# An attention kernel with sparse experts: visits of four value tiles beside six ring banks, the expert table shared with GpSimd, and expert down products one slot later

## The reference

```python
Q, K, V = heads(layernorm(x) @ W_Q), heads(ctx @ W_K), heads(ctx @ W_V)
attn = softmax(where(mask == 0, -1e9, Q @ K.T / sqrt(d)))
x = x + tanh(g0) * (merge(attn @ V) @ W_T)
h = layernorm(x)
w, sel = top_k(softmax(h @ router_w.T), 2)
y = sum over the two chosen experts e of w_e * ((silu(h @ gate_e) * (h @ up_e)) @ down_e)
x = x + tanh(g1) * y
```

## Time and profile before

| | us |
|---|---|
| median of 3 runs | 448.39 |
| lowest and highest run | 444.69, 450.77 |
| profiled execution | 447.15 |
| span of its trace, first to last instruction | 445.0 |

### The profile page before, as it was taken

How to read it: one execution, slowest core, us unless ns; L and a number is a source line. 1 busy time by engine, 2 the same in 40 slices (tenths; PEclk the granted TensorE clock), 3 DMA queues, 4 the chain that set the end, 5 groups by cost and what they waited for, 6 DMA issues and landing times. The chain is left out here.

```text
span 445.0 us, 10141 instructions
## 1 busy us (share of the span) xinstructions
PE 409.3 (92%) x3747; PEld 237.4 (53%) x3747; DVE 323.0 (73%) x698; ACT 273.3 (61%) x576; POOL 118.7 (27%) x260
## 2 busy tenths in 40 slices
PE   7887999999999999999999999999984877989996
PEld 3436455555564555555555555545532556666785
DVE  3980778677777899888889988888991662432786
ACT  3302656676776777777777777777761557645433
POOL 4815653436342115000111500101130000000176
PEclk9988999999999999999999999999995999999999
DMA  8866935449557640413314052240414123655112
GB/s 285 167 156 128 214 118 118 166 98 340 144 147 259 158 98 25 97 35 67 87 25 98 26 98 48 53 98 13 97 30 163 55 78 109 165 156 153 39 47 71
DMA packets 31805, 50.35 MB, mean 113 GB/s; under 512 B 3612, under 2 KB 20188, under 8 KB 31756
## 3 DMA queue, kind: packets, MB, share of 16 engines
q1 hardware_dynamic: 29684, 47.53, 42.0%
q0 software_dynamic: 768, 1.57, 1.2%
q10 hardware_dynamic: 1304, 0.59, 0.5%
HBM read 36.00 MB, written 13.44 MB: 111 GB/s over the span
## 5 line engine op out<-in xcount | busy, mean ns | idle before, releaser
L1041 DVE TENSOR_REDUCE chunk_max<-banks 128x1 f32<-128x512 f32 (+1 forms) x390 | 239.6, 664 | 72.0 <-PE banks L1440 70.6
L886 ACT ACTIVATE probs<-banks 128x512 f32<-128x512 f32 x384 | 210.4, 601 | 75.3 <-PE banks L1458 74.9
L1458 PE MATMUL banks<-queries,keys 75*128 75x256 bf16 (+1 forms) x832 | 158.2, 274 | 2.1 <-DVE chunk_max L1041 1.1
L1440 PE MATMUL banks<-keys,queries 72*128 72x512 bf16 x480 | 145.1, 335 | 1.3 <-DVE chunk_max L1041 1.0
L1458 PEld LDWEIGHTS banks<-queries,keys 75*128 75x128 bf16 (+1 forms) x832 | 72.0, 100 | 75.3 <-issue 16.1
L1483 PE MATMUL banks<-probs,value_t 128*9 128x256 f32 x1536 | 98.4, 382 | 0.0
L1483 PEld LDWEIGHTS banks<-probs,value_t 128*9 128x9 f32 x1536 | 34.8, 90 | 45.3 <-ACT probs L886 11.6
L1440 PEld LDWEIGHTS banks<-keys,queries 72*128 72x128 bf16 x480 | 42.3, 97 | 13.7 <-DVE chunk_max L1041 4.2
L646 POOL COPY value_t<-values 128x384 f32<-128x384 f32 x16 | 8.1, 504 | 122.8 <-PE banks L1483 119.5
L1239 DVE SCALAR_TENSOR_TENSOR late<-late,banks 128x256 f32<-128x256 f32 x35 | 14.5, 416 | 22.0 <-ACT late L910 21.4
L910 ACT ACTIVATE late<-banks 128x256 f32<-128x256 f32 x35 | 13.4, 384 | 25.3 <-PE banks L1530 14.3
(11 more groups left out here) (178 smaller groups left out, 360.4 us busy)
## 6 DMA issues: line engine op xcount, KB each, us to landing
keys<-k_parts SPq DMA_DIRECT2D x48, 300.2 KB
keys<-w SPq DMA_DIRECT2D x19, 384.0 KB, 3.3
slot_x<-ctx_in SPq DMA_DIRECT2D x5, 704.0 KB, 4.7
ctx_in<-ctxT SPq DMA_DIRECT2D x3, 800.5 KB, 11.3
k_parts<-split SPq DMA_DIRECT2D x6, 400.2 KB, 9.2
k_parts<-late SPq DMA_DIRECT2D x6, 400.2 KB, 7.2
queries<-q_parts SPq DMA_DIRECT2D x16, 144.0 KB
w<-w SPq DMA_DIRECT2D x1, 2048.0 KB, 13.0
```

What stands on the lines that cost most here:

```text
L886: nc.scalar.activation(probs[:, s % (HELD * QH), :], ring[ring_bank["scores", n]][:, :], ACT.Exp, scale=SCALE).then_inc(probs_ready, 1)
L1041: nc.vector.reduce_max(dst, src, axis=AX.X).then_inc(chunk_used, 1)
L1440: last = nc.tensor.matmul(dst[:, i * CW[c]:(i + 1) * CW[c]], queries[q][0:ROWS, j, t * P:(t + 1) * P], keys[q][0:ROWS, j, c * BANK:c * BAN ...
L1458: last = nc.tensor.matmul(dst, keys[q][0:KR, j, t * P:t * P + w], queries[q][0:KR, j, :], start=True, stop=not with_mask)
```

## The change

Four things are altered.

1. `visit(u)` gives four value tiles in units 5 to 7 and 9 to 11 as well. The ring keeps its six banks there.
2. The table of unit 13: the five sums and comparisons stay on DVE, in slots 4 to 8 (`table_sums`); the other six steps go to POOL (`table`), ahead of the scatter of batch 2.
3. SP's first loads in unit 13 are two tiles' weights and three tiles' rows, then, in slots 19 to 25, two more weights and eight more rows in between (`FIRST_LOADS`); there are 11 row buffers in place of 3.
4. `SPARSE_AT`: the down products of 12 tiles move, ten of them one slot later, tile 0's by two and tile 4's by four, and four tiles of unit 15 are turned or multiplied up one or two slots earlier.

```diff
-S_TABLE = (5, 6, 7, 8, 10, 11, 12, 13, 14, 15, 16)
+S_SUMS = (4, 5, 6, 7, 8)
-S_SLOT_LOADS, S_ROW_LOADS, S_NEG_LOAD = 16, 17, 18
+S_NEG_LOAD = 18
+FIRST_LOADS = {13: "ww", 15: "rrr", 19: "w", 21: "rr", 22: "w", 24: "rrr", 25: "rrr"}
-W_BUFS, ROW_BUFS, XT_BUFS, Y_BUFS = 4, 3, 2, 4
+W_BUFS, ROW_BUFS, XT_BUFS, Y_BUFS = 4, 11, 2, 4
-SPARSE_AT = [(FIRST_SPARSE, 20, 22, 23, 26, 6), (FIRST_SPARSE, 24, 26, 27, 30, 6),
-             (FIRST_SPARSE + 1, 2, 4, 5, 11, 6), (FIRST_SPARSE + 1, 6, 8, 9, 12, 6), (FIRST_SPARSE + 1, 10, 12, 13, 15, 6),
+SPARSE_AT = [(FIRST_SPARSE, 20, 22, 23, 28, 6), (FIRST_SPARSE, 24, 26, 27, 31, 6),
+             (FIRST_SPARSE + 1, 2, 4, 5, 11, 6), (FIRST_SPARSE + 1, 6, 8, 9, 13, 6), (FIRST_SPARSE + 1, 10, 12, 13, 19, 6),
...
 def visit(u):
 
-    return 2 if NQ <= u <= FIRST_SPARSE else 4
+    return 2 if u >= NQ and u % NQ == 0 or u == FIRST_SPARSE else 4
...
+            def table():
+
+                pool.wait_ge(table_step, 2)
+                nc.gpsimd.tensor_tensor(ends_in[:, :, :], upto[:, :, :], tiles_of[:, None, :].broadcast_to([P, E, E]),
+                                        ALU.mult).then_inc(table_step, 1)
+                nc.gpsimd.tensor_scalar(short_of[:, :], tiles_of[0:1, :], -1.0, float(MOST), ALU.mult, ALU.add).then_inc(short_ready, 1)
+                pool.wait_ge(short_ready, 1)
+                pool.wait_ge(table_step, 5)
+                nc.gpsimd.tensor_tensor(passed_short[:, :, :], passed[:, :, :], short_of[:, None, :].broadcast_to([1, NS, E]),
+                                        ALU.mult).then_inc(short_ready, 1)
+                pool.wait_ge(table_step, 6)
+                nc.gpsimd.tensor_scalar(expert_i[:, :], expert_f[:, :], float(E - 1), None, ALU.min).then_inc(table_ready, 1)
+                pool.wait_ge(table_step, 7)
+                steps = Chain(pool, table_step, 7)
+                steps.link(nc.gpsimd.tensor_tensor(row_f[:, :], row_f[:, :], tile_f[:, :], ALU.add))
+                nc.gpsimd.tensor_scalar(row_i[:, :], row_f[:, :], float(P), None, ALU.mult).then_inc(table_ready, 1)
...
+                        if tail and q == 1 and b == SPARSE and s == S_SCATTER:
+                            table()
                         if tail and q == 1 and b <= SPARSE and s == S_SCATTER:
                             scatter(b)
...
+            def table_sums(step):
+
+                if step == 2:
+                    dve.wait_ge(table_step, 4)
+                    nc.vector.tensor_tensor(passed[:, :, :], ends[0:1, None, :].broadcast_to([1, NS, E]),
+                                            tile_f[:, :, None].broadcast_to([1, NS, E]), ALU.is_le).then_inc(table_step, 1)
+                    return
+                target, src, after = ((tiles_of[:, :], full[:, :, :], 1), (ends[:, :], ends_in[:, :, :], 3), None,
+                                      (expert_f[:, :], passed[:, :, :], 5), (row_f[:, :], passed_short[:, :, :], 6))[step]
+                dve.wait_ge(table_step, after)
+                if step == 4:
+                    dve.wait_ge(short_ready, 2)
+                nc.vector.reduce_sum(target, src, axis=AX.X).then_inc(table_step, 1)
```

More of the change, by code:

```diff
@@ L345, in block_kernel @@
         ends = sb("ends", [P, E], FP32)
-        passed = sb("passed", [1, NS, E], FP32)
+        passed, passed_short = sb("passed", [1, NS, E], FP32), sb("passed_short", [1, NS, E], FP32)
         expert_f = sb("expert_f", [1, NS], FP32)
@@ L444, in block_kernel @@
         scattered, table_step, table_ready = sem("scattered"), sem("table_step"), sem("table_ready")
[L445 removed]
+        shift_step, y_place_ready, short_ready = sem("shift_step"), sem("y_place_ready"), sem("short_ready")
         pick_step, picks_ready = sem("pick_step"), sem("picks_ready")
@@ L573, in sparse_slot @@
             def sparse_slot(u, s):
-                if (u, s) == (FIRST_SPARSE, S_SLOT_LOADS):
-                    sp.wait_ge(scores_ready, SLOTS * FIRST_SPARSE)
-                    sp.wait_ge(table_ready, 2)
-                    for i in range(W_BUFS):
-                        load_slot_weights(i)
-                if (u, s) == (FIRST_SPARSE, S_ROW_LOADS):
-                    sp.wait_ge(scattered, 16 * SPARSE * COLS)
-                    for i in range(ROW_BUFS):
+                if u == FIRST_SPARSE and s in FIRST_LOADS:
+                    if s == min(FIRST_LOADS):
+                        sp.wait_ge(scores_ready, SLOTS * FIRST_SPARSE)
+                        sp.wait_ge(table_ready, 2)
+                    done = "".join(what for at, what in FIRST_LOADS.items() if at < s)
+                    for n, what in enumerate(FIRST_LOADS[s]):
+                        i = done.count(what) + FIRST_LOADS[s][:n].count(what)
+                        if what == "w":
+                            load_slot_weights(i)
+                            continue
+                        if i == 0:
+                            sp.wait_ge(scattered, 16 * SPARSE * COLS)
                         load_rows(i)
@@ L1165, in places @@
                     nc.vector.tensor_copy(place_i[:, COLS * (b - 1):COLS * b], place_f[:, COLS * (b - 1):COLS * b]).then_inc(place_ready, 1)
-            def tables(step):
-                steps = Chain(dve, table_step, 1 + step)
-                if step == 0:
-                    dve.wait_ge(table_step, 1)
-                    steps.link(nc.vector.reduce_sum(tiles_of[:, :], full[:, :, :], axis=AX.X))
-                if step == 1:
-                    steps.link(nc.vector.tensor_tensor(ends_in[:, :, :], upto[:, :, :], tiles_of[:, None, :].broadcast_to([P, E, E]),
-                                                       ALU.mult))
-                if step == 2:
-                    steps.link(nc.vector.reduce_sum(ends[:, :], ends_in[:, :, :], axis=AX.X))
-                if step == 3:
-                    steps.link(nc.vector.tensor_tensor(passed[:, :, :], ends[0:1, None, :].broadcast_to([1, NS, E]),
-                                                       tile_f[:, :, None].broadcast_to([1, NS, E]), ALU.is_le))
-                if step == 4:
-                    steps.link(nc.vector.reduce_sum(expert_f[:, :], passed[:, :, :], axis=AX.X))
-                if step == 5:
-                    steps.link(nc.vector.tensor_scalar(short_of[:, :], tiles_of[0:1, :], -1.0, float(MOST), ALU.mult, ALU.add))
-                if step == 6:
-                    steps.link(nc.vector.tensor_tensor(passed[:, :, :], passed[:, :, :], short_of[:, None, :].broadcast_to([1, NS, E]),
-                                                       ALU.mult))
-                if step == 7:
-                    steps.link(nc.vector.reduce_sum(row_f[:, :], passed[:, :, :], axis=AX.X))
-                if step == 8:
-                    steps.link(nc.vector.tensor_tensor(row_f[:, :], row_f[:, :], tile_f[:, :], ALU.add))
-                if step == 9:
-                    nc.vector.tensor_scalar(row_i[:, :], row_f[:, :], float(P), None, ALU.mult).then_inc(table_ready, 1)
-                if step == 10:
-                    nc.vector.tensor_scalar(expert_i[:, :], expert_f[:, :], float(E - 1), None, ALU.min).then_inc(table_ready, 1)
@@ L1197, in y_places @@
-            def y_places(step):
+            def table_sums(step):
[10 more added lines that the diff above has]
+                nc.vector.reduce_sum(target, src, axis=AX.X).then_inc(table_step, 1)
@@ L1199, in y_places @@
+            def y_places(step):
+                if step == 0:
+                    dve.wait_ge(table_ready, 2)
                 steps = Chain(dve, shift_step, step)
@@ L1278, in units @@
                                 places(b, S_POS.index(s))
-                            if b == SPARSE and s in S_TABLE:
-                                for step, at in enumerate(S_TABLE):
-                                    if at == s:
-                                        tables(step)
+                            if b == SPARSE and s in S_SUMS:
+                                table_sums(S_SUMS.index(s))
                         if u == LATE_UNIT and s in S_Y_PLACES:
```

11 lines of the change are left out of this document (5 added, 6 removed).

## The result

The changed kernel takes 443.42 us (median of 20 runs, 437.17 to 448.13), the kernel before beside it 448.69 (20 runs, 444.05 to 455.09). The ratio is **0.9865, 95% interval 0.9825 to 0.9906**: 1.35% faster. It compares the means of the runs in the faster of two states, 11 of each kernel, where the medians of all 20 would give 0.988.

A forecast was written before the change was run, and what follows sets the result against it. PE sets the pace in units 5 to 7 and 9 to 11; in unit 13 the table ends PE's wait for rows. 447.15 + 5.3 - 5.0 - 1.2 - 2.6 - 2.0 = 441.6 us, range 439.5 to 444.5 (0.58).

The forecast's parts named there:

- Part 1: Units 5 to 7 and 9 to 11: visits of four tiles make PE wait for DVE's chunks; +5.3 us.
- Part 2, the table: Unit 13: with table steps on POOL the table ends sooner and the first turn comes earlier; -5.0 us.
- Part 2, the clock: Unit 13: half of the time lost to half clock behind the first turn comes back; -1.2 us, bounds -2.4 and 0.
- Part 3: Rows and weights loaded ahead in unit 13: the loads stay hidden and bring nothing.
- Part 4: Later down products fill or avoid PE's waits: -2.6 us in unit 14, -2.0 us in unit 15.
- The rise by 0.6 us: Unit 13: by the skill's rule on GpSimd's speed, POOL's four-step chain ends later and the time is 442.2.
- (a): Rival for units 5 to 7 and 9 to 11: the longer visits gain; time 432.7, chance 0.12.
- its mixture: Rival: the sixth bank relieves more than worked out, longer visits cost about +1 us; time 437.3, chance 0.14.
- (b): Rival: DVE doesn't catch up between visits, each of 18 stretches costs 0.8 us; time 452.1, chance 0.04.
- (c): Rival: scatter or rows land late, the clock falls as before, down products bring half; time 446.2, chance 0.12.

The follow-up runs named there:

- e8: The changed kernel with visits of two tiles and the whole table on DVE in slots 4 to 8, none on POOL; 438.84 us.
- e3: The changed kernel with five ring banks in all units, so long visits without the sixth bank; 463.15 us in one run.
- e7: The kernel before with only the new slots of the expert tiles; 441.00 us, ratio 0.9841.
- e9: The changed kernel with visits of two, eight table steps on DVE, three on POOL behind the scatter, first rows loaded ahead of weights; 434.73 us, ratio 0.9650.
- e6: The changed kernel with the expert slots and the visits of two tiles of the kernel before, so only the table and early loads; 443.35 us.
- e11: The kernel of e9 with visits of two tiles in units 1 to 3 as well; 432.05 us, ratio 0.9644.
- e10: The kernel of e1 run once more, unchanged, in another series; 439.06 us, ratio 0.9840.
- e1: The changed kernel with two value tiles a visit again in units 5 to 7 and 9 to 11; 443.87 us, ratio 0.9715.
- e4: The changed kernel with each chunk's maximum on DVE taken over half of its columns, leaving out computation; 444.36 us in one run.
- e5: The changed kernel itself, run again on another chip; 441.21 us, ratio 0.9788 to the kernel before.
- part 1 alone: The kernel before with only visits of four tiles in units 5 to 7 and 9 to 11, run twice; 467.83 and 471.27 us.
- the first and fourth series: Two of four groups of follow-up runs, each with the kernel before on the same chip; there it took 458.21 and 461.56 us.
- e2: The kernel before with only four value tiles a visit in units 5 to 7 and 9 to 11; 467.83 us, ratio 1.0225.

## Why the prediction was right

The forecast was 441.6 us against a profiled execution of 447.15; the profiled execution of the changed kernel took 441.74, and the ratio of 0.9865 lies beside the 1.2% that had been worked out. That the sum is so close is partly luck: the clock and the last stretch came out 1.65 and 0.6 us worse than forecast, unit 15, the first turn and part 1 0.8, 0.5 and 0.3 better, and 0.4 us less lay outside the span. The runs of the changed kernel spread over 11 us, so that the profiled one lies within 0.2 us of the forecast is luck too.

**Part 1: +5.3 forecast, +5.04 measured.** The working holds term by term. The stretch of slots 18 to 25 is 4.11 us as worked out. In unit 6, slots 18 to 25 are longer by 0.28 us (0.30 forecast), slots 10 to 17 by 0.32 (0.35), and slots 0 to 9 shorter by 0.05 (0). Units 5 and 9 pay 0.87 more, in slots 7 and 8 (1.17 and 0.90 us where PE needs 0.44 and 0.66), for the rows' places; 0.7 was taken. The three experiments on it change different things: going back to two tiles restores 18.72, five banks give 20.03, half of DVE's work gives 18.24. The rule of the Trainium skill (Perfetto Trace Analysis, section Matmul Optimizations), that matmuls should run back to back in batches, was read as one for longer visits, which would have been the -3.6. Here the longer visits gain only where DVE's maxima are made shorter (18.24 us), and the granted clock of unit 6 is 1.00 with either kind of visit.

**Part 2, the table: first turn -5.0 forecast, -5.5 measured.** Less the shift of the unit's start (4.91 us), the table ends at 325.1 (325.5 forecast), the last transfer goes out at 329.5 (329.5), it lands at 332.2 (331.7), the rows are issued at 333.0 (332.8) and land at 334.7 (335.2). The link that was sized worst is the landing of the scatter, 2.73 us against 2.2; the rows' 1.7 us against 2.4 more than made up for it. The wait in slot 17 is 1.51 us (1.9), that for the rows 0.96 (1.7). POOL's steps, taken at 0.3 each, took 0.19 to 0.50: 0.50 for the 1x152 product that took DVE 0.30 in e8, 0.32 for the 128x64 one that took DVE 0.21. For element by element work the Trainium skill (GPSIMD Engine Reference, section Performance versus the Vector engine) has GpSimd at half the speed, and these two rows give 1.5 and 1.7 times the duration. The rise by 0.6 us that was worked out from it didn't come: the table ended 0.4 us sooner than forecast, since the two slow products lie between DVE's steps and not behind them.

**Part 2, the clock: -1.2 forecast, +0.45 measured.** This is the step that failed. The clock's stretch at half is shorter by 3.4 us (6.8 in place of 10.2), but what was cut off was idle time: before, it began at 334.7, 5.5 us ahead of the turn, in the wait itself; now it begins 1.2 us ahead of it. Behind the turn PE runs at half for 5.7 us now and for 4.7 before, and from the turn to the unit's end it needs 9.56 us in place of 9.11. The bound of no gain at all was too narrow by this much. With the same instructions and no fall the unit takes 25.51, with 3.4 us of it 27.07, with 6.8 us 27.76 and 28.01, and 28.47 in e3. So the gain that was forecast exists in some runs and not in others.

**Part 3: nothing, and nothing measured.** In unit 14 nothing waits for weights or rows, and e7 has the same 29.37 us with the old loads. In e9, whose unit 13 is shorter, PE waits 0.7 us for weights in unit 14.

**Part 4: unit 14 -2.6, measured -2.61; unit 15 -2.0, measured -2.78.** In unit 14 the wait for ACT's copy (1.1 us) is gone, and PE's waits ahead of turns fall from 4.3 us to 1.9, while its busy time rises by 0.8. That fits down products that fill those waits; the prediction was wrong only in saying that the waits ahead of turns stay. In unit 15 I had kept to part of the 2.7 us of gate waits, since one slot gives a down product only 0.22 us of cover. Only three of the four waits, 2.3 us, stand in unit 15, and all three are gone; the fourth, 0.3 us, stands behind the unit in both kernels. The 2.78 is just beyond the bound of 2.7 that was given. What brings the rest, beyond the three waits, no run separates; four tiles are also turned or multiplied up sooner.

**Not foreseen:** the last stretch, +0.6 us. It is 39.0 in e6 to e9 and e11 and 39.8 to 40.1 in the changed kernel, its second run and e10. It arises behind all computing: DVE's last step ends 36.8 us into the stretch with the change and 36.9 before, and what is longer is the last transfer of `out`, from issue to landing 2.6 us in place of 1.8. The clock isn't the cause, for it falls to half at 437.4, after PE's last product. That transfer takes 2.6 to 2.9 us in all six profiles that have both the table ahead of the scatter and the new expert slots (the changed kernel, e1, e3, e4, e5, e10), and 1.8 in the other eight. What delays it there is open.

**The rivals.** (a), a gain of the longer visits, is refuted by e1 and e4, and its mixture, which gave part 1 about +1 us, by the +5.04. (b), 0.8 us a stretch, is refuted for the stretch itself, but the whole kernel with part 1 alone came out 2.3% and 3.4% slower in the first and fourth series, for the reason told there: a rival that I hadn't named, a pause in units 5 and 9, gives the sign of (b) by another way. Whether the changed kernel as a whole is still faster than before under that condition wasn't measured. As an estimate, e1's 443.87 us and the 10.6 us by which units 5 to 7 and 9 to 11 of e2 are longer than e1's give 454.5, against 458.21 for the kernel before in that series. (c) is refuted for the table's wait, whose turn comes 5.5 us sooner, and for the expert slots; that the clock gives nothing back came true.

## What to carry to other kernels

When a long batch on one engine takes the place of two short ones, look at what must be produced or drained between two batches, and by whom: the short batch had been the time in which DVE caught up, and the longer one brought its 0.2 us only where DVE's work was cut (e4). A sixth bank gave 0.22 us a stretch and wasn't enough; a deeper ring wasn't run. Work that is moved to another engine's queue delays what stands behind it there: the table ahead of the scatter made the scatter the late one, and with the table behind it and the first rows loaded sooner (e9) the unit took 23.4 us, where it took 25.5 without a fall of the clock and 28.0 with one. A stretch at half clock costs only where the engine works in it, so a shorter wait ahead of it need not bring any of it back.

## What the runs showed of the hardware

- The clock's fall isn't a property of the program alone. Twenty runs of the changed kernel spread from 437.17 to 448.13 us, and one and the same unit 13 has 0, 3.4 or 6.8 us at half clock. Nor do PE's waits in that unit alone decide it. Between 13 and 19 us into the unit, e1 and e3 have the same three waits of 0.95, 0.24 and 1.1 us and 0.94, 0.25 and 1.0 us: in e1 the clock doesn't fall, in e3 it falls 18.4 us into the unit, for 6.8. The changed kernel and e10 have two, 1.51 and 0.96 us and 1.51 and 1.06: the clock falls in the one 17.3 us into the unit, ahead of the second wait, for 6.8, in the other at 19.3, behind it, for 3.4. The order of e9, in which PE waits for neither, had no fall in its profile, and means of 0.987 to 0.998 over its six runs.
- In the first and fourth series the last stretch takes 48.3 to 50.2 us, in the others 39.0 to 40.1. In it POOL issues twelve indirect transfers in a row, 1.25 us apart in both cases. ACT in the last stretch of e1, behind the last three of them (to 422.3):

```profile
424.48 0.66 ACT L934 ACTIVATE late<-banks 128x256 f32<-128x256 f32 x2 [7.38 <-remote]
```

  "Remote" is a releaser that the profile doesn't know. DVE then waits 6.30 us for ACT; in e10 none of its waits at this place is over 0.52. As in units 5 and 9, ACT and DVE with work at hand stand still in these two series while indirect transfers are issued and up to 2.2 us beyond; in the others the same transfers are issued without it. What holds them back, no row shows, and it stays open.
- The last transfer of `out`, 128 KB from SBUF to HBM, lands 1.8 us after its issue in eight profiles and 2.6 to 2.9 in six, and alike in every kernel with the same table and expert slots.
